# Three rotating PSUM banks each for scores and for transposed scores in the exact attentions of a four-layer cross-attention kernel

## The chip, the cores and the metric

The kernel runs on one core of a Trainium2 chip. The metric is the device time of one execution in microseconds (us): 1616.45 us before the change, the median of three runs that lie between 1616.28 and 1617.36. Five engines work side by side and meet only at semaphores: TensorE (PE; its weight loads are a row of their own, PEld), VectorE (DVE), ScalarE (ACT), GpSimd (POOL) and SyncE (SP), which here only issues transfers. PSUM, into which TensorE writes, has eight banks of 512 fp32 values per partition.

## The reference

A batch of four sequences of 512 tokens, 128 features wide, goes through four layers, and each layer also attends to a context of 154 rows. The change touches the three "exact" attentions, which have 16 heads of 8 features:

```python
# layer 0: cross attention with a padding mask over the 154 context rows
# layer 1: causal self attention over 512 tokens, then cross attention to the context
scores = jnp.einsum('bqhd,bkhd->bhqk', Q, Kp) / jnp.sqrt(jnp.float32(HD))
if causal:
    scores = jnp.where(mask, scores, -jnp.inf)
a = jax.nn.softmax(scores, axis=-1)
o = jnp.einsum('bhqk,bkhd->bqhd', a, V).reshape(Bq, Sq, Dm)
return o @ wo + bo
```

What follows (a mixture of experts, two attentions on 8-bit codes, a gated feed-forward, a grouped attention with rotary positions and a last feed-forward) is left as it is.

## The kernel before

Work on the exact attentions is cut into 12 units, one sequence of one attention each: units 0 to 3 are the padded cross attention (L0), 4 to 7 the causal self attention, 8 to 11 the second cross attention. A unit has 4 groups of 4 heads.

The scores are computed twice. First with queries on the partitions, only to find the maximum of each row: this is a **score step** (`scores_exact` on PE, `top_exact` on DVE), which covers two heads and one tile of 128 queries (two tiles in a cross unit). A cross unit has 16 of them and a self unit 32; in a self unit the widths fall, because of the causal mask, from 512 keys per head over 384 and 256 to 128. All in all there are 256 steps. PE writes the two heads of a step to the two banks of `score[0]` or `score[1]`, in turn, and then counts up `scores_ready`. DVE takes the maximum over both heads in one `tensor_reduce` (line 1960) and counts up `top_ready`. Before step s PE waits until the maximum of step s-2 is taken (line 1099).

Then the scores are computed again with keys on the partitions and the negative maxima added by a further matmul (`scores_transposed`). One **block** is 128 x 512 such transposed scores in one bank of `trans`; a cross group has 5 blocks and a self group 10. PE makes the blocks in pairs w and w+1 (the fifth of a cross group by itself, lines 1137 and 1139), and ACT takes the exponential of each block (line 1509) and counts up `expT_ready`. Before a pair PE waits until the exponentials of all blocks before w are done (line 1130). `weigh_batch` (lines 1175 and 1177) then multiplies the exponentials by the values.

The order is written out by hand. PE, ACT and DVE walk over the same slots, one for each block. PE does in slot w: the transposed pair if w is even within its group, the score steps that `STEPS_OF_SLOT` puts there (they are those of the next group), the items of the slot, and the weighing of a finished batch. In a self group of ten slots the steps stand in slots 8 and 9 (512 keys per head), 0 and 1 (384), 3 and 4 (256) and 5 and 6 (128), so that three times in a group two steps follow each other on PE without a pair between them: in slots 8 and 9, 0 and 1, and 4 and 5. In a cross group of five slots they stand in slots 3 and 4 and in 0 and 1.

Items are the projections and norms of the units around: `K`, `Q`, `V` are projections, `N1`, `r` and `N2` the inversion of the sums (four reciprocals on DVE, line 1727) and the product with them (line 1731), `W` the output projection, then the row statistics on DVE (lines 1633 to 1643), a power on POOL (line 2134), `M` the normalisation on DVE (line 1659) and `H` its transposition (line 941). `tops` transposes the maxima of a group (line 989). The stacked queries and keys of the next unit go through DRAM and come back by transfers that SP issues (lines 800 to 818); the first score step of a unit waits for them.

Of the kernel before, what the change touches and what calls it, by code (L numbers as in the profile page):

```python
# [7 lines left out]
P = 128  # L8
# [387 lines left out]
def build(nc, io, out):  # L396
# [3 lines left out]
    with ctx:  # L400
# [173 lines left out]

        score = [ctx.enter_context(nc.psum_tensor(f"score{i}", [P, 2, 512], fp32)) for i in range(2)]
        trans_pair = ctx.enter_context(nc.psum_tensor("trans", [P, 2, 512], fp32))
        trans = [trans_pair[:, i, :] for i in range(2)]
        acc = ctx.enter_context(nc.psum_tensor("acc", [P, 512], fp32))
        misc = ctx.enter_context(nc.psum_tensor("misc", [P, 512], fp32))
# [203 lines left out]
        with nc.Block() as block:  # L783
# [145 lines left out]
            def _(pe):  # L929
# [152 lines left out]
                def scores_exact(u, i):  # L1082
# [13 lines left out]
                    if u == 0 and i == PER_GROUP[0]:  # L1096
                        pe.wait_ge(q_stacked, 32 * len(Q_TERMS))
                    if at_step >= 2:
                        pe.wait_ge(top_ready, at_step - 1)

                    banks = [(half_rows(s), score[at_step % 2][:, s, :]) for s in range(2)]
                    if is_cross(u):
                        for j in range(2):
                            t, of = 2 * n + j, slice(j * CTX, (j + 1) * CTX)
                            for r, bank in banks:
                                ins = nc.tensor.matmul(bank[:, of], q_stack[r, u % 2, c, t * P:(t + 1) * P],  # L1106
                                                       k_stack_ctx[r, u % 2, c, 0:CTX], start=True, stop=(stage(u) != L0))
                            if stage(u) == L0:
                                for r, bank in banks:
                                    ins = nc.tensor.matmul(bank[:, of], ones_pad[r, :], pad_rows[r, u % 2, :],  # L1110
                                                           start=False, stop=True)
                    else:
                        width = P * (n + 1)
                        for r, bank in banks:
                            nc.tensor.matmul(bank[:, 0:width], q_stack[r, u % 2, c, n * P:(n + 1) * P],
                                             k_stack[r, u % 2, c, 0:width], start=True, stop=False)
                        for h in range(2):
                            for r, bank in banks:
                                ins = nc.tensor.matmul(bank[:, width - P:width], unit_halves[r, h, :], causal[r, h, :],
                                                       start=False, stop=(h == 1))  # L1120
                    ins.then_inc(scores_ready, 1)

                def scores_transposed(w):
# [5 lines left out]
                    if w >= 2:  # L1129
                        pe.wait_ge(expT_ready, blocks[-1] - 1)  # L1130
                    if w == 0 or BLOCKS[w - 1][1] != g:
                        pe.wait_ge(misc_read, out_of("tops", u, g))
                    if len(blocks) == 1:
                        bank = trans[w % 2]
                        pe.wait_ge(k_tail_ready, seq(u) + 1 + (B if stage(u) == CROSS else 0))
# [6 lines left out]
                    for n in range(len(pieces)):  # L1142
                        _, k, q0, c0 = pieces[n]

                        two = [(j, half_rows(j % 2), 2 * g + j // 2, trans[z % 2][:, c0:c0 + TOKENS - q0])
                               for z in blocks for j in [BLOCKS[z][3][n][0]]]
# [80 lines left out]

                pe.wait_ge(top_ready, EXACT_STEPS)
                pe.wait_ge(expT_ready, EXACT_SLOTS)
# [169 lines left out]
            def _(act):  # L1399
# [96 lines left out]
                for w, (u, g, _, pieces) in enumerate(BLOCKS):  # L1496
# [10 lines left out]
                    if n == 0 and stage(u) == L0:  # L1507
                        act.wait_ge(pad_ready, u + 1)
                    nc.scalar.activation(expT[w % SLOTS], trans[w % 2][:, :], ACT.Exp, bias=bias)\  # L1509
                        .then_inc(expT_ready, 1)  # L1510
# [112 lines left out]
            def _(dve):  # L1623
# [326 lines left out]
                def top_exact(u, i):  # L1950
                    c, n = exact_steps(u)[i]
                    at_step = STEP_BASE[u] + i
                    dve.wait_ge(scores_ready, at_step + 1)
                    tops = minus_top[:, :].rearrange("p (t h) -> p h t", h=HEADS)[:, 2 * c:2 * c + 2, :]
                    if is_cross(u):
                        dst = tops[:, :, 2 * n:2 * n + 2]
                        src = score[at_step % 2][:, :, 0:2 * CTX].rearrange("p s (j k) -> p s j k", j=2)
                    else:
                        dst, src = tops[:, :, n], score[at_step % 2][:, :, 0:P * (n + 1)]
                    nc.vector.tensor_reduce(dst, src, axis=AX.X, op=ALU.max, negate=True).then_inc(top_ready, 1)  # L1960

                def split_tops(u, g):
# [3 lines left out]
                    to = top_cols[:, g % 2, :, :, :].rearrange("p t (s z) c -> p t z s c", s=2)  # L1966
                    dve.wait_ge(top_ready, STEP_BASE[u] + PER_GROUP[u] * (g + 1))
                    if GROUPS * u + g >= 2:
# [155 lines left out]
            def _(pool):  # L2124
# [15 lines left out]
                def item(name, u, n=None):  # L2140
# [10 lines left out]
                    elif name == "pads":  # L2151
# [6 lines left out]
                        if b >= 2:  # L2158
                            pool.wait_ge(top_ready, STEP_BASE[b - 1])
                        then(nc.gpsimd.tensor_scalar(pad_col_add[:, b, :], pad_col[:, b, :], -1.0, 1.0e10, ALU.add, ALU.mult))  # L2160
# [205 lines left out]
```

## Time and profile before

| | |
|---|---|
| median of three runs | 1616.45 us |
| the profiled execution | 1629.24 us |
| its span | 1627.4 us |
| exact attentions | about 33 to 594 us of the span |
| of these the self units | about 205 to 432 us |
| score steps (maxima on DVE) | 256 |
| blocks (exponentials on ACT) | 320 |

The profiled execution is 1.84 us longer than its span, which is what lies around it, and 12.8 us (0.8%) longer than the median. PE is the busiest engine in the exact attentions; DVE is second. After 594 us none of the changed lines runs. In a row of the timeline the first number is the start, the second how long the row's instructions took from the first start to the last end, and what stands in brackets is how long the engine had been idle before and who released it.

### The profile page before, as it was taken

What the parts mean: (1) busy time and instruction counts of PE and PEld (TensorE: products, weight loads), DVE (VectorE), ACT (ScalarE), POOL (GpSimd) and SP (SyncE); (2) the same over time, 40 slices, a digit from 0 to 9 for tenths busy, and PEclk for the clock granted to TensorE, in tenths of its full rate; (3) what the DMA queues carried; (4) which work ended last, traced back from release to release, by engine and by line L of the source; (5) the groups of instructions that cost most, each with busy time, mean ns of one, the idle gap of its engine ahead of it and who ended that gap; (6) DMA issues with size and microseconds to landing.
All of it is one profiled execution on the core that took longest, in us unless ns stands there. A gap on an engine that the chain in (4) does not pass through costs nothing.

```text
span 1627.4 us, 28786 instructions
## 1 busy us (share of the span) xinstructions
PE 1109.7 (68%) x9344; PEld 600.2 (37%) x9344; DVE 1109.3 (68%) x3126; ACT 895.0 (55%) x2546; POOL 681.6 (42%) x1054
## 2 busy tenths in 40 slices
PE   2688888787777679784435354444439787898888
PEld 1333344444322238681111121122215544453545
DVE  2577777777666666277989899877765556666533
ACT  1344455545543346347767688888872344545542
POOL 3321010111011323456888888877771245354420
PEclk9899999999998999796555555555559889999999
DMA  6223242022172111217546566655650112111000
GB/s 175 62 47 72 49 120 92 10 72 48 32 150 42 35 41 52 74 40 182 116 95 111 97 110 118 120 109 107 106 106 1 26 40 53 33 28 46 3 1 26
DMA packets 263829, 115.86 MB, mean 71 GB/s; under 512 B 216056, under 2 KB 252544, under 8 KB 261504
## 3 DMA queue, kind: packets, MB, share of 16 engines
q1 hardware_dynamic: 258720, 107.61, 31.6%
q0 software_dynamic: 2048, 4.20, 0.9%
q10 hardware_dynamic: 2912, 2.22, 0.5%
q8 instruction: 75, 1.23, 0.3%
q14 instruction: 74, 0.61, 0.1%
HBM read 38.80 MB, written 16.45 MB: 34 GB/s over the span
## 4 chain that ended last, share of the span: by engine, by line
PE 35%; POOL 19%; issue 17%; DVE 15%; ACT 10%; DMA 2%; SPq 1%; POOLq 0%; another core or an unknown queue 0%; ACTq 0%; DVEq 0%
POOL arena L2268 10%; ACT arena L1562 5%; PE acc L1177 3%; PE trans L1149 2%; POOL inv_total L2257 2%; PE misc L999 2%; PE misc L1005 2%; PE trans L1301 2%; ACT arena L1509 2%; POOL arena L2215 2%; PE score L1313 2%; PE score L1315 2%; PE trans L1155 2%; PE acc L1175 1%; DVE arena L1727 1%
## 5 line engine op out<-in xcount | busy, mean ns | idle before, releaser
L2268 POOL TENSOR_SCALAR arena<-arena,inv_total 128x512 f16<-128x512 f32 (+1 forms) x512 | 302.6, 591 | 55.8 <-DVE inv_total L2038 15.4
L1960 DVE TENSOR_REDUCE minus_top<-score 128x4 f32<-128x616 f32 (+4 forms) x256 | 201.4, 803 | 140.9 <-PE score L1110 54.6
L2134 POOL TENSOR_TENSOR rstd<-spread,minus_half 128x4 f32<-128x4 f32 x36 | 37.7, 1048 | 526.1 <-DVE spread L1643 456.9
L1562 ACT ACTIVATE arena<-score,minus_top,exp_scale 128x512 f32<-128x512 f32 (+1 forms) x340 | 210.6, 626 | 18.1 <-POOL arena L2268 8.1
L1509 ACT ACTIVATE arena<-trans 128x512 f32<-128x512 f32 x240 | 134.5, 596 | 113.8 <-PE trans L1155 107.8
L1600 ACT ACTIVATE arena<-arena,minus_top 128x154 f32<-128x154 f32 x256 | 105.1, 412 | 133.0 <-DVE minus_top L2103 132.9
L1258 PE MATMUL score<-arena 32*128 32x512 bf16 (+1 forms) x340 | 69.0, 458 | 144.1 <-ACT arena L1562 143.2
L2044 DVE TENSOR_REDUCE top_score<-score 128x2 f32<-128x1024 f32 (+1 forms) x128 | 135.7, 1061 | 0.6 <-PE score L1258 0.5
L2288 POOL TENSOR_TENSOR arena<-arena,inv_total 128x512 f32<-128x512 f32 x64 | 66.7, 1041 | 147.4 <-DVE inv_total L2111 133.6
L1562 ACT ACTIVATE arena<-trans,minus_top,exp_scale 128x154 f32<-128x154 f32 (+1 forms) x172 | 105.6, 621 | 16.2 <-POOL arena L2268 11.8
L2098 DVE CUSTOM_DVE_ANT_0 arena<-score,arena 128x154 f32<-128x154 f32 x256 | 66.0, 314 | 62.8 <-PE score L1338 62.4
L2027 DVE TENSOR_SCALAR arena<-arena 128x1024 bf16<-128x1024 f16 x192 | 102.7, 535 | 5.5 <-DMA arena<-arena 5.5
L1553 ACT ACTIVATE minus_top<-top_score,exp_scale 128x2 f32<-128x2 f32 (+1 forms) x192 | 56.5, 294 | 61.4 <-DVE top_score L2044 61.1
L1258 PEld LDWEIGHTS score<-arena 32*128 32x128 bf16 x340 | 14.3, 102 | 195.4 <-ACT arena L1562 178.0
L1177 PE MATMUL acc<-arena 128*32 128x512 f32 (+3 forms) x768 | 80.6, 507 | 4.7 <-issue 4.0
L1258 PE MATMUL trans<-arena 32*128 32x154 bf16 (+1 forms) x172 | 34.7, 451 | 72.0 <-ACT arena L1562 71.8
L1106 PE MATMUL score<-arena 64*128 64x154 bf16 x512 | 45.7, 248 | 54.0 <-issue 32.7
L1527 ACT ACTIVATE arena<-score,arena 128x128 f32<-128x128 f32 x184 | 52.0, 372 | 50.4 <-PE score L1214 43.4
L1277 PE MATMUL acc<-arena 128*32 128x128 bf16 x1536 | 59.2, 307 | 27.8 <-DVE oT L2052 15.2
L1509 ACT ACTIVATE arena<-trans,arena 128x512 f32<-128x512 f32 x80 | 52.3, 687 | 30.6 <-PE trans L1155 27.0
L2044 DVE TENSOR_REDUCE top_score<-trans 128x2 f32<-128x1024 f32 (+1 forms) x64 | 67.4, 1053 | 0.0
L1447 ACT COPY arena<-misc 128x512 bf16<-128x512 bf16 x48 | 28.1, 586 | 70.1 <-PE misc L989 67.3
(282 smaller groups left out, 2902.6 us busy)
## 6 DMA issues: line engine op xcount, KB each, us to landing
arena<-q_terms SPq DMA_DIRECT2D x176, 64.0 KB
late<-arena SPq DMA_DIRECT2D x128, 64.0 KB, 2.0
q_terms<-arena SPq DMA_DIRECT2D x36, 128.0 KB
late<-k_terms SPq DMA_DIRECT2D x64, 64.0 KB
arena<-arena SPq DMA_TRANSPOSE x192, 3.1
by_expert<-zeros SPq DMA_DIRECT2D x2, 1472.0 KB, 17.6
arena<-by_expert SPq DMA_DIRECT2D x10, 256.0 KB, 3.0
from_expert<-arena SPq DMA_DIRECT2D x10, 256.0 KB
```

The lines of the kernel that those rows point to most:

```text
L1177: ins = nc.tensor.matmul(acc[32 * j:32 * j + 32, q0:TOKENS], v_cols[:, k, 4 * g + j, :], src, start=(b % half == 0 and k == 0), stop=(last ...
L1258: ins = nc.tensor.matmul(quant_score[i % 3][:, j, z * n:(z + 1) * n], qT_codes[r:r + 32, u % 2, t * P:(t + 1) * P], k4_codes[r:r + 32, u % ...
L1277: ins = nc.tensor.matmul(acc[32 * j:32 * j + 32, P * t:P * (t + 1)], vals[:, 4 * j + i, :], pT_codes[:, (2 * n + j // 2) % CODE_SLOTS, j % ...
L1509: nc.scalar.activation(expT[w % SLOTS], trans[w % 2][:, :], ACT.Exp, bias=bias)\
L1562: ins = nc.scalar.activation(probs[:, i % 3, j, of], quant_score[i % 3][:, j, of], ACT.Exp, bias=minus_top[:, at_col:at_col + 1], scale=ex ...
L1600: ins = nc.scalar.activation(gq_exp_p[:, i % 3, h, :], shifted[:, i % 3, h, :], ACT.Exp, bias=minus_top[:, at_col:at_col + 1], accum_out=t ...
L1960: nc.vector.tensor_reduce(dst, src, axis=AX.X, op=ALU.max, negate=True).then_inc(top_ready, 1)
L2027: nc.vector.tensor_scalar(pT_codes[:, of, :, :].rearrange("p k q -> p (k q)"), pT_raised[:, of, :, :].rearrange("p k q -> p (k q)"), -HALF ...
L2044: nc.vector.tensor_reduce(of_step(top_score, i), src, axis=AX.X, op=ALU.max, negate=True).then_inc(quant_top, 1)
L2098: ins = nc.vector.tensor_tensor_reduce(out=shifted[:, i % 3, h, :], in0=score[i % 2][:, odd, z * CTX:(z + 1) * CTX], in1=mask_add[:, b % 2 ...
L2268: ins = nc.gpsimd.tensor_scalar(codes[:, (i - 1) % CODE_SOURCES, j, to], probs[:, (i - 1) % 3, j, of], inv_total[:, at_col:at_col + 1], HA ...
L2288: nc.gpsimd.tensor_tensor(gq_p[:, v % 2, :, :], gq_exp_p[:, v % 3, :, 0:P], inv.to_broadcast([P, 4, P]), ALU.mult)
```

## The change

The six banks of `score` and `trans` become one tensor of six banks, and the other stages go on using the same places in it. In the exact attentions the split is now 3 and 3. Head h of the running count of heads (two per step) goes to score bank h mod 3, and block w to transposed bank w mod 3. DVE takes a maximum for each head by itself, 512 `tensor_reduce` in place of 256, and `top_ready` counts heads. PE makes both heads of a step as before and signals once. Before step s it waits for `2 * at_step - 1` maxima, which is up to and including the first head of step s-1. Before a pair it waits for one exponential fewer than before.

```diff
-        score = [ctx.enter_context(nc.psum_tensor(f"score{i}", [P, 2, 512], fp32)) for i in range(2)]
-        trans_pair = ctx.enter_context(nc.psum_tensor("trans", [P, 2, 512], fp32))
+        banks = ctx.enter_context(nc.psum_tensor("banks", [P, 6, 512], fp32))
+        score = [banks[:, 2 * i:2 * i + 2, :] for i in range(2)]
+        trans_pair = banks[:, 4:6, :]
         trans = [trans_pair[:, i, :] for i in range(2)]
+        score_bank = [banks[:, i, :] for i in range(3)]
+        trans_bank = [banks[:, 3 + i, :] for i in range(3)]
...
-                    if at_step >= 2:
-                        pe.wait_ge(top_ready, at_step - 1)
-                    banks = [(half_rows(s), score[at_step % 2][:, s, :]) for s in range(2)]
+                    if at_step:
+                        pe.wait_ge(top_ready, 2 * at_step - 1)
+                    heads = [(half_rows(s), score_bank[(2 * at_step + s) % 3]) for s in range(2)]
...
                     if w >= 2:
-                        pe.wait_ge(expT_ready, blocks[-1] - 1)
+                        pe.wait_ge(expT_ready, blocks[-1] - 2)
...
-                        two = [(j, half_rows(j % 2), 2 * g + j // 2, trans[z % 2][:, c0:c0 + TOKENS - q0])
+                        two = [(j, half_rows(j % 2), 2 * g + j // 2, trans_bank[z % 3][:, c0:c0 + TOKENS - q0])
...
-                    nc.scalar.activation(expT[w % SLOTS], trans[w % 2][:, :], ACT.Exp, bias=bias)\
+                    nc.scalar.activation(expT[w % SLOTS], trans_bank[w % 3], ACT.Exp, bias=bias)\
...
-                    if is_cross(u):
-                        dst = tops[:, :, 2 * n:2 * n + 2]
-                        src = score[at_step % 2][:, :, 0:2 * CTX].rearrange("p s (j k) -> p s j k", j=2)
-                    else:
-                        dst, src = tops[:, :, n], score[at_step % 2][:, :, 0:P * (n + 1)]
-                    nc.vector.tensor_reduce(dst, src, axis=AX.X, op=ALU.max, negate=True).then_inc(top_ready, 1)
+                    for s in range(2):
+                        bank = score_bank[(2 * at_step + s) % 3]
+                        if is_cross(u):
+                            dst, src = tops[:, s, 2 * n:2 * n + 2], bank[:, 0:2 * CTX].rearrange("p (j k) -> p j k", j=2)
+                        else:
+                            dst, src = tops[:, s, n:n + 1], bank[:, 0:P * (n + 1)]
+                        nc.vector.tensor_reduce(dst, src, axis=AX.X, op=ALU.max, negate=True).then_inc(top_ready, 1)
```

The other waits on `top_ready` are only recounted (all heads of the same steps as before). On PE no instruction is added, removed or moved. On DVE every maximum becomes two. This is DVE in a self unit, from the reciprocals of the unit before to the statistics of its output, before the change (`late` and `arena` are SBUF areas, `score` the PSUM banks):

```order
L1727 RECIPROCAL arena<-arena 128x128 [waits misc_read] x2
L1960 TENSOR_REDUCE minus_top<-score 128x2 [waits scores_ready]
L1727 RECIPROCAL arena<-arena 128x128 [waits misc_read]
L1960 TENSOR_REDUCE minus_top<-score 128x2 [waits scores_ready]
L1731 TENSOR_TENSOR oT<-misc,arena 128x512 [waits sums_inverted,misc_raised]
L1960 TENSOR_REDUCE minus_top<-score 128x2 [waits scores_ready]
L1739 TENSOR_TENSOR y<-misc,x 128x512 [waits x_ready,misc_raised]
```

And the same place after it:

```order
L1733 RECIPROCAL arena<-arena 128x128 [waits misc_read] x2
L1967 TENSOR_REDUCE minus_top<-banks 128x1 [waits scores_ready]
L1967 TENSOR_REDUCE minus_top<-banks 128x1
L1733 RECIPROCAL arena<-arena 128x128 [waits misc_read]
L1967 TENSOR_REDUCE minus_top<-banks 128x1 [waits scores_ready]
L1967 TENSOR_REDUCE minus_top<-banks 128x1
L1737 TENSOR_TENSOR oT<-misc,arena 128x512 [waits sums_inverted,misc_raised]
L1967 TENSOR_REDUCE minus_top<-banks 128x1 [waits scores_ready]
L1967 TENSOR_REDUCE minus_top<-banks 128x1
L1745 TENSOR_TENSOR y<-misc,x 128x512 [waits x_ready,misc_raised]
```

The order of the work is the same; each reduction stands as two of one column each, the second without a wait.

## Rows read from the trace of the kernel before

**Rows 1.** Stretches: length, busy PE, PEld, DVE, ACT, POOL; clock, DMA share, GB/s.

```profile
205.00:432.00 227.00, 183.19 (x2494) 96.22 (x2494) 167.35 (x362) 119.35 (x220) 18.17 (x20) 0.99 0.23 61
33.00:205.00 172.00, 134.10 (x1074) 58.45 (x1070) 112.97 (x256) 76.48 (x129) 33.36 (x57) 0.90 0.30 60
432.00:594.00 162.00, 118.12 (x747) 46.43 (x743) 107.15 (x334) 66.61 (x127) 33.20 (x40) 0.91 0.34 72
```

**Rows 2.** Waits of PE in the self units (205 to 432 us).

```profile
PE trans L1149 <- ACT arena L1509: 25.2, 27, 1.2
```

**Rows 3.** Waits of PE in the cross units, 33 to 205 and 432 to 594 us.

```profile
PE score L1106 <- issue: 14.0, 3, 6.4
...
PE score L1106 <- issue: 18.7, 3, 7.3
```

**Rows 4.** Groups by line and shape, the maxima: count, busy us, mean ns.

```profile
L1960 DVE TENSOR_REDUCE minus_top<-score 128x2 f32<-128x1024 f32 x32 | 37.7, 1205 | 11.7 <-PE score L1119 11.7
...
L1960 DVE TENSOR_REDUCE minus_top<-score 128x2 f32<-128x512 f32 x32 | 21.6, 688 | 12.6 <-PE score L1119 12.4
L1960 DVE TENSOR_REDUCE minus_top<-score 128x2 f32<-128x256 f32 x32 | 13.4, 420 | 11.5 <-PE score L1119 11.3
```

**Rows 5.** Timeline of one self group, 305 to 317 us.

```profile
305.36 0.28 PE L1119 MATMUL score<-masks 64*128 64x128 bf16 x4
...
305.68 2.36 DVE L1960 TENSOR_REDUCE minus_top<-score 128x2 f32<-128x1024 f32 x2 [0.80 <-PE score L1119]
305.90 0.39 PE L1115 MATMUL score<-late,arena 64*128 64x512 bf16 x2
...
308.05 0.28 PE L1119 MATMUL score<-masks 64*128 64x128 bf16 x4
...
308.16 0.33 PE L1115 MATMUL score<-late,arena 64*128 64x384 bf16 x2
...
309.99 1.09 ACT L1509 ACTIVATE arena<-trans 128x512 f32<-128x512 f32 x2 [0.81 <-PE trans L1155]
311.13 0.34 PE L1149 MATMUL trans<-arena,late 64*128 64x384 bf16 x2 [0.96 <-ACT arena L1509]
...
311.91 0.28 PE L1119 MATMUL score<-masks 64*128 64x128 bf16 x4
...
312.02 0.22 PE L1115 MATMUL score<-late,arena 64*128 64x128 bf16 x2
...
315.30 0.28 PE L1149 MATMUL trans<-arena,late 64*128 64x256 bf16 x2 [1.01 <-ACT arena L1509]
...
316.72 0.39 PE L1115 MATMUL score<-late,arena 64*128 64x512 bf16 x2
```

**Rows 6.** Timeline where DVE's items precede the maxima, 278 to 290 us.

```profile
278.38 0.39 PE L1115 MATMUL score<-late,arena 64*128 64x512 bf16 x2
...
278.92 1.16 DVE L1960 TENSOR_REDUCE minus_top<-score 128x2 f32<-128x1024 f32 x1
...
287.58 0.27 PE L1115 MATMUL score<-late,arena 64*128 64x256 bf16 x2
...
288.53 1.28 DVE L1960 TENSOR_REDUCE minus_top<-score 128x2 f32<-128x512 f32 x2
...
288.76 0.63 PE L941 MATMUL misc<-ident,normed 128*128 128x128 f32 x4 [0.80 <-DVE normed L1659]
...
289.32 0.10 PEld L1115 LDWEIGHTS score<-late,arena 64*128 64x128 bf16 x2 [0.17 <-DVE minus_top L1960]
```

**Rows 7.** Timeline of a cross unit behind its transfer wait, 460 to 470 us.

```profile
460.50 0.44 PE L1106 MATMUL score<-arena 64*128 64x154 bf16 x4 [7.31 <-issue]
...
464.55 0.43 PE L1106 MATMUL score<-arena 64*128 64x154 bf16 x8
464.89 1.51 DVE L1960 TENSOR_REDUCE minus_top<-score 128x4 f32<-128x616 f32 x2 [0.92 <-PE score L1106]
...
469.77 0.39 PE L1149 MATMUL trans<-arena 64*128 64x512 bf16 x2 [0.45 <-ACT arena L1509]
```

More of the change, by code:

```diff
@@ L1104, in scores_exact @@
                             t, of = 2 * n + j, slice(j * CTX, (j + 1) * CTX)
-                            for r, bank in banks:
+                            for r, bank in heads:
                                 ins = nc.tensor.matmul(bank[:, of], q_stack[r, u % 2, c, t * P:(t + 1) * P],
@@ L1108, in scores_exact @@
                             if stage(u) == L0:
-                                for r, bank in banks:
+                                for r, bank in heads:
                                     ins = nc.tensor.matmul(bank[:, of], ones_pad[r, :], pad_rows[r, u % 2, :],
@@ L1113, in scores_exact @@
                         width = P * (n + 1)
-                        for r, bank in banks:
+                        for r, bank in heads:
                             nc.tensor.matmul(bank[:, 0:width], q_stack[r, u % 2, c, n * P:(n + 1) * P],
@@ L1117, in scores_exact @@
                         for h in range(2):
-                            for r, bank in banks:
+                            for r, bank in heads:
                                 ins = nc.tensor.matmul(bank[:, width - P:width], unit_halves[r, h, :], causal[r, h, :],
@@ L1133, in scores_transposed @@
                     if len(blocks) == 1:
-                        bank = trans[w % 2]
+                        bank = trans_bank[w % 3]
                         pe.wait_ge(k_tail_ready, seq(u) + 1 + (B if stage(u) == CROSS else 0))
@@ L1226, in down @@
                     ins.then_inc(down_raised, 1)
-                pe.wait_ge(top_ready, EXACT_STEPS)
+                pe.wait_ge(top_ready, 2 * EXACT_STEPS)
                 pe.wait_ge(expT_ready, EXACT_SLOTS)
@@ L1966, in split_tops @@
                     to = top_cols[:, g % 2, :, :, :].rearrange("p t (s z) c -> p t z s c", s=2)
-                    dve.wait_ge(top_ready, STEP_BASE[u] + PER_GROUP[u] * (g + 1))
+                    dve.wait_ge(top_ready, 2 * (STEP_BASE[u] + PER_GROUP[u] * (g + 1)))
                     if GROUPS * u + g >= 2:
@@ L2158, in item @@
                         if b >= 2:
-                            pool.wait_ge(top_ready, STEP_BASE[b - 1])
+                            pool.wait_ge(top_ready, 2 * STEP_BASE[b - 1])
                         then(nc.gpsimd.tensor_scalar(pad_col_add[:, b, :], pad_col[:, b, :], -1.0, 1.0e10, ALU.add, ALU.mult))
```

## The prediction

> **What bounds the kernel now.** The changed lines run only in the exact attentions, so busy shares over the whole span decide nothing, and I read the busy time by stretch first. PE is busy 183.2 of 227 us in the self units (81%), 78% in the L0 units and 73% in the second cross attention; DVE is busy 74%, 66% and 66% [rows 1]. PE walks its list in order, so what it waits for is what a gain must come from. The waits by line give that directly: in the self units PE stands 25.2 us, 27 times, in front of a transposed pair until ACT has finished the exponentials [rows 2]. In the cross units the large entry is another: three waits of 14.0 us and three of 18.7 us in all in front of a score step [rows 3]. The profile only calls them "issue", but each is the first step of a unit, behind which the stacked keys and queries come back from DRAM, so I take them for waits on transfers. The timeline of one self group shows the pattern. It comes again after 10.82 us (the step at 305.90 and the one at 316.72), and in it the pairs at 311.13 and at 315.30 stand 0.96 and 1.01 us waiting, the other three in the group do not stand [rows 5].
>
> **What the third transposed bank gives.** A pair now needs one exponential fewer. Two exponentials in a row take 1.09 us, so one is 0.54 us [rows 5]. A pair that stood 0.96 or 1.01 us will stand about 0.45. In all self units this gives at most 27 times 0.54 = 14.6 us, for the 27 waits of [rows 2]. Not all of it arrives. In the second group of each unit the pairs follow on H and W items that are themselves late (below), so I count four pairs a unit in groups three and four and none in the second: 4 x 0.54 = 2.2 us a unit. In the first group one pair stands too, but the next thing that PE needs is a maximum for which DVE is late anyway (278.92 [rows 6]), so that gain is lost.
>
> **What the third score bank costs.** Here the count of banks misleads. Before, two steps could be in flight, in four banks. Now a step still fills two banks and there are three, so a step shares a bank with the step directly before it. PE must wait until DVE has taken the first maximum of that step. Where a pair, a batch or a large item stands between two steps this is hidden; where two steps are neighbours it is not. The wait is: DVE starts 0.04 us after the last matmul of the first step (305.36 + 0.28 = 305.64 against 305.68 [rows 5]), takes the first head, and PE gets going again 0.10 us after the end of a maximum (288.53 + 0.69 = 289.22 against the weight load at 289.32, with 688 ns for that shape [rows 4, 6]).
>
> One head of 512 keys is the size of the 128x512 row, 0.69 us; of 256 keys the 128x256 row, 0.42 us; 384 keys lie halfway, 0.55 us [rows 4]. So:
> - Slots 8 and 9, 512 keys: the next step starts at 305.64 + 0.04 + 0.69 + 0.10 = 306.47 in place of 305.90: +0.57.
> - Slots 0 and 1, 384 keys: 308.33 + 0.69 = 309.02 in place of 308.16: +0.86.
> - Slots 4 and 5, 256 keys: 312.19 + 0.56 = 312.75 in place of 312.02: +0.73.
>
> The ends of matmuls are modelled, and the first part of a step overlapped with the one before, so the lower bound of each takes off 0.08, 0.24 and 0.18: 0.49, 0.62 and 0.55. A plain self group then pays 1.66 to 2.16 us and gets back 1.08. It becomes 0.6 to 1.1 us longer, on 10.8.
>
> Counted for a unit of four groups: in slots 4 and 5 of the first group the V item lies between the steps, in slots 10 and 11 the W item, in 14 and 15 H, and slots 8 and 9 of the first group are priced in the next part. There remain three neighbours of 512 keys, three of 384 and two of 256, in total 3 x 0.57 + 3 x 0.86 + 2 x 0.73 = 5.75 us, or 4.4 us at the lower prices.
>
> **Where DVE is late.** In the second group DVE has reciprocals, a product and the row statistics between the maxima. The second step of 512 keys started at 278.38, while the first maximum did not start before 278.92 [rows 6]. After the change it has to wait until 278.92 + 0.69 + 0.10 = 279.71: +1.33 us. What stands behind it on PE is the N2 item, and behind that the product on DVE, the W item, the statistics, POOL's power, the normalisation and H, one chain. Further on, the step at 287.58 will need the first half of the maximum that started at 288.53: 288.53 + 0.42 + 0.10 = 289.05, then its own 0.3 us, so H, which is in line behind it, starts at 289.35 or later and not at 288.76: +0.6. Together 1.9 us, of which I take 1.8, since part of the second lateness is the first one seen again; bounds 1.2 and 2.3.
>
> **The split itself.** Two maxima of half the size take longer than one: 2 x 0.688 - 1.205 = 0.17 us and 2 x 0.420 - 0.688 = 0.15 us [rows 4]. For 256 steps that is 41 us of DVE. In the self units DVE rises from 167.4 to 188 of 227 us (83%), still beside PE. Its price is in the chain above only where DVE is late; I take 0.1 us a unit in addition. At worst, were DVE the bound, all 20 us of the self units would count. The Trainium skill ("Perfetto Trace Analysis", section "Optimizing Scalar/DVE Operations") gives about 125 ns of fixed cost for a DVE instruction that reads PSUM, and the trace's 150 to 170 ns is near it and decides.
>
> **Self units.** 5.75 + 1.8 + 0.1 - 2.2 = 5.4 us a unit at the upper prices, and 4.4 + 1.2 - 2.2 = 3.4 at the lower. I take 4.5, 18 us for four units, with ends at 13 and 24 (the last with the 2.3).
>
> **Cross units.** What PE does ahead of the wait for transfers is free in both directions, up to the 7.31 us of the row at 460.50 [rows 7]. What counts is from there to the next unit's Q item. There one neighbouring couple of steps (464.55, both in one row of 8 matmuls) will pay: DVE starts at 464.89, one head of 2 x 154 values takes 0.49 us (a line through 256 and 512 values [rows 4]), 464.89 + 0.49 + 0.10 = 465.48 against a second step that began about 464.7: +0.8. The pair at 469.77 waited 0.45 us for an exponential, and that goes [rows 7]. With 0.1 us more on DVE before the parts of Q this is +0.3 to +0.4 a unit, and 2 us for the seven units (bounds 0 and 5). Unit 0 has the same couples with nothing to win at the start: +1. Unit 11 has hardly any steps left and only wins: -1.
>
> **Sum.** 18 + 2 + 1 - 1 = +20 us. It is made against the profiled execution of 1629.24 us (span 1627.4 and 1.84 around it). The median of the runs is 0.8% shorter, which changes 20 us by 0.2, so: 1616.45 + 20 = 1636.
>
> **Against this speaks a rule.** The Trainium skill ("Perfetto Trace Analysis", sections "Optimization Strategy" and "Optimizing Scalar/DVE Operations") says that a gap that keeps returning on the engine that should be full can mean too little PSUM for the next tile, and that breaking up an instruction of an engine that is not full may let others go on sooner. For the pairs the trace agrees (0.96 and 1.01 us each time). For the scores there are no such gaps of PE now, so there is nothing that a maximum per head could give back.
>
> **The rivals.**
> - *The pairs win.* If the new stalls of the steps fall where PE would have stood for ACT anyway, and the third bank gives what it can: 14.6 us from [rows 2] less some 5 us of stalls that stay. That would be 1616 - 10 = 1606. For it speaks that PE's largest wait is this one. Against it speaks the order: between slots 0 and 1 and the pair that stood (slot 4) lie a batch and a full pair, and ACT starts later by as much as that pair does. This is the rule above as a mechanism. 0.10.
> - *Even.* Stalls of steps are at the lower prices, DVE's chain in the second group hides its own lateness, and all five standing pairs a unit win: 4 x (4.4 - 2.7) = 7, less what the first group absorbs, 4 to 7, gives 0 to 3 us: 1618. 0.07.
> - *DVE becomes the bound in the self units.* It decides once PE's stalls push DVE's items behind the maxima so that both wait for each other through the whole unit: the 20 us of the split come on top of half of the rest, +32: 1648. For it speaks 83% busy with an in-order list; against it, that DVE still idles before most maxima of a plain group (0.80 us at 305.68 [rows 5]). 0.10.
> - *The score rotation does nothing.* One signal for both heads could make three banks as good as two steps in flight, if DVE were always ahead. The couples of [rows 5] exclude it: DVE cannot take a maximum before it is there. Chance 0.
>
> **How the numbers follow.** The forecast has 0.73, with a range of its own of 1627 to 1646. A change under 0.2% (3.2 us) cannot be told from none here. Faster 0.10, within 0.07, slower 0.83. The range for 8 in 10 leaves out the pairs' victory and the far half of the case of DVE: 1617 to 1648.
>
> **What would show it.** Right: the waits list of PE gains an entry of score steps on DVE's maxima of 25 to 40 us with some 50 or more waits, and the entry of pairs on ACT falls from 25.2 to 10 to 14 us in the self units; the self units as a whole grow by 13 to 24 us, and a plain group goes from 10.8 to between 11.4 and 11.9; the maxima are 512 with 20% more busy time; nothing changes behind 594 us but the start. Wrong: if plain groups stay at 10.8, the neighbours are covered by something that I did not see; if DVE no longer idles before maxima in plain groups, it is the bound; if the cross units shift by more than 1 us each, the transfer wait was not the limit there.

## The result, and the profile after

The changed kernel takes 1646.67 us (median of four runs, 1645.34 to 1656.61); the kernel before, timed beside it, 1616.37 us. The ratio is 1.0191, with an interval of 1.0150 to 1.0231. Timed again it was 1.0152 (1.0091 to 1.0214). Some executions of a kernel are slower as a whole; ratios and the differences of medians leave them out, among them one of the changed kernel at 3471.51 us. The change makes the kernel slower, as forecast; the forecast of 1636 us had +20 us in it, the medians show +30 and +25, and the two profiled executions lie 16.1 us apart (1629.24 and 1645.34).

Where the time went is read from three starts of the profile after: the first score step, the first transposition of the experts (the end of the exact attentions) and the first score of the quantised attention behind the experts. Columns are start, length, engine, line, operation, output and inputs.

```profile
32.29 0.31 PE L1111 MATMUL banks<-arena 64*128 64x154 bf16 x2 [15.29 <-DMA arena<-q_terms]
615.59 0.63 PE L1210 MATMUL acc<-ident,arena 128*128 128x128 f32 x4 [0.77 <-ACT arena L1491]
753.35 0.61 PE L1264 MATMUL banks<-arena 32*128 32x512 bf16 x6 [0.70 <-issue]
```

Before, the same three stand at 32.68, 597.12 and 736.88. From the first to the second it was 564.4 us and is now 583.3: +18.9. From the second to the third it was 139.8 and is 137.8. So the loss lies in the exact attentions, and the stages behind them give nothing to it. Within, I use one length for all kernels from here on, the **self stretch**: from the start of the pair in slot 0 of the first self unit to the last full pair of the fourth. It is 214.7 us before (205.25 to 419.98), 214.7 in a second profile of the kernel before, 233.1 after (208.89 to 442.02) and 235.8 in a second profile of the changed kernel. So +18.4 and +21.0 stand there.

What PE waited for in the exact attentions after the change, by line (in total, times, longest):

```profile
PE banks L1120 <- DVE minus_top L1967: 35.2, 45, 1.7
PE banks L1111 <- DMA arena<-q_terms: 31.0, 4, 15.3
PE banks L1111 <- DVE minus_top L1967: 22.4, 35, 1.6
PE banks L1111 <- issue: 14.0, 2, 9.7
PE banks L1155 <- ACT arena L1515: 10.4, 20, 0.7
```

L1120 and L1111 are score steps (self and cross), L1155 the pairs. The entry that [rows 2] had, 25.2 us of pairs in front of ACT, has fallen to 10.4. In its place stand 35.2 us of self steps in front of a maximum, and 22.4 us in cross units. The transfer waits of [rows 3] are still there, partly under another name (q_terms).

The maxima, which were [rows 4], by shape (busy us, mean ns of one, then the idle time before them):

```profile
L1967 DVE TENSOR_REDUCE minus_top<-banks 128x2 f32<-128x308 f32 x256 | 109.1, 468 | 89.8 <-PE banks L1115 53.7 <-PE banks L1111 35.5
L1967 DVE TENSOR_REDUCE minus_top<-banks 128x1 f32<-128x512 f32 x64 | 40.7, 677 | 5.1 <-PE banks L1124 4.9
L1967 DVE TENSOR_REDUCE minus_top<-banks 128x1 f32<-128x384 f32 x64 | 32.7, 552 | 14.4 <-PE banks L1124 13.5
L1967 DVE TENSOR_REDUCE minus_top<-banks 128x1 f32<-128x256 f32 x64 | 24.1, 418 | 12.2 <-PE banks L1124 12.2
L1967 DVE TENSOR_REDUCE minus_top<-banks 128x1 f32<-128x128 f32 x64 | 15.5, 284 | 15.4 <-PE banks L1124 14.5
```

One head's duration is what the forecast took (0.69, 0.55 and 0.42 us against 677, 552 and 418 ns). But 64 times 677 ns is 43.3 us and the busy time is 40.7: two maxima in a row overlap. All of them are busy 222.0 us against 201.4 before, 10% more and not 20%. DVE idles before every shape, so it isn't the bound.

A plain self group after, the rows of PE in which it stood (they answer to [rows 5]; the number in brackets is the wait):

```profile
312.85 0.34 PE L1155 MATMUL banks<-arena,late 64*128 64x384 bf16 x2 [0.47 <-ACT arena L1515]
314.43 0.23 PE L1120 MATMUL banks<-late,arena 64*128 64x128 bf16 x2 [0.53 <-DVE minus_top L1967]
317.22 0.28 PE L1155 MATMUL banks<-arena,late 64*128 64x256 bf16 x2 [0.53 <-ACT arena L1515]
319.18 0.39 PE L1120 MATMUL banks<-late,arena 64*128 64x512 bf16 x2 [0.46 <-DVE minus_top L1967]
322.26 0.34 PE L1120 MATMUL banks<-late,arena 64*128 64x384 bf16 x2 [0.66 <-DVE minus_top L1967]
324.62 0.34 PE L1155 MATMUL banks<-arena,late 64*128 64x384 bf16 x2 [0.47 <-ACT arena L1515]
```

From one group's pair to the next group's it is 11.77 us against 10.82. The pairs stand 0.47 and 0.53 in place of 0.96 and 1.01, and the second step of each of the three couples (slots 4 and 5, 8 and 9, 0 and 1) stands 0.53, 0.46 and 0.66 us where none stood.

The place in the first group where DVE is late ([rows 6] shows it before), now:

```profile
285.66 0.28 PE L1155 MATMUL banks<-arena,late 64*128 64x256 bf16 x2 [0.53 <-ACT arena L1515]
288.86 0.39 PE L1120 MATMUL banks<-late,arena 64*128 64x512 bf16 x2 [1.70 <-DVE minus_top L1967]
289.29 3.00 PE L1003 MATMUL misc<-arena 128*128 128x512 f32 x4
292.22 1.69 PE L1183 MATMUL acc<-arena 128*32 128x384 f32 x16
```

And the same stretch in windows (PE busy, weight loads, DVE, ACT, POOL, then the granted clock, DMA share, GB/s):

```profile
287.00:289.00 2.00, 0.30 (x5) 0.11 (x4) 2.00 (x4) 1.22 (x3) 0.00 (x0) 1.00 0.52 135
289.00:291.00 2.00, 2.00 (x9) 0.92 (x6) 2.00 (x4) 0.00 (x0) 0.00 (x0) 0.78 0.51 139
291.00:293.00 2.00, 2.00 (x10) 0.34 (x12) 1.06 (x2) 0.00 (x0) 0.00 (x0) 0.50 0.52 139
293.00:295.00 2.00, 2.00 (x32) 0.95 (x25) 0.14 (x2) 0.40 (x1) 0.00 (x0) 0.87 0.51 135
```

PE works 0.30 us of the two before 289, and then the granted clock falls from 1.00 to 0.50 (from the 2.4 to the 1.2 GHz level). The N2 item and the batch behind it take 3.00 and 1.69 us here. The same place in the first self unit of the same profile has the same wait, and there the clock stays at 1.00 and they take 1.98 and 1.07:

```profile
228.28 0.39 PE L1120 MATMUL banks<-late,arena 64*128 64x512 bf16 x2 [1.70 <-DVE minus_top L1967]
228.71 1.98 PE L1003 MATMUL misc<-arena 128*128 128x512 f32 x4
230.62 1.07 PE L1183 MATMUL acc<-arena 128*32 128x384 f32 x16
```

Of the four waits of 1.70 us in this profile the second and the third are followed by a fall of the clock, the first and the fourth are not. The forecast had not priced this.

### The profile page after: what moved, and what is told of

It is laid out like the page before. It is cut to its first block, busy times and chain, and to the rows that moved or that the text cites. A ratio compares the mean times of both kernels' runs of the same rounds, so it can differ in the third digit from the quotient of the medians.

```text
span 1643.5 us, 29042 instructions
## 1 busy us (share of the span) xinstructions
PE 1112.0 (68%) x9344; PEld 594.9 (36%) x9344; DVE 1127.2 (69%) x3382; ACT 893.9 (54%) x2546; POOL 679.7 (41%) x1054
## 4 chain that ended last, share of the span: by engine, by line
PE 34%; POOL 19%; DVE 18%; issue 14%; ACT 9%; DMA 4%; SPq 2%; POOLq 0%; DVEq 0%; ACTq 0%
POOL arena L2275 10%; ACT arena L1568 5%; DVE minus_top L1967 3%; PE acc L1183 3%; DMA arena<-q_terms 3%; POOL inv_total L2264 2%; PE misc L1003 2%; PE misc L1009 2%; PE banks L1155 2%; PE banks L1307 2%; PE banks L1319 2%; PE banks L1321 2%; DVE top_score L2051 1%; SPq L811 1%; PE banks L1120 1%
## 5 line engine op out<-in xcount | busy, mean ns | idle before, releaser
L1568 ACT ACTIVATE arena<-banks,minus_top,exp_scale 128x512 f32<-128x512 f32 (+1 forms) x512 | 315.9, 624 | 33.9 <-POOL arena L2275 19.3
L1967 DVE TENSOR_REDUCE minus_top<-banks 128x2 f32<-128x308 f32 (+4 forms) x512 | 222.0, 476 | 136.9 <-PE banks L1115 53.7
L1264 PE MATMUL banks<-arena 32*128 32x512 bf16 (+1 forms) x512 | 101.8, 455 | 215.3 <-ACT arena L1568 214.0
L1515 ACT ACTIVATE arena<-banks 128x512 f32<-128x512 f32 x240 | 134.5, 596 | 130.4 <-PE banks L1161 125.7
L2051 DVE TENSOR_REDUCE top_score<-banks 128x2 f32<-128x1024 f32 (+1 forms) x192 | 203.1, 1058 | 0.6 <-PE banks L1264 0.5
L2105 DVE CUSTOM_DVE_ANT_0 arena<-banks,arena 128x154 f32<-128x154 f32 x256 | 65.9, 313 | 58.0 <-PE banks L1344 57.5
L1568 ACT ACTIVATION_READ_ACCUMULATOR arena<-banks,minus_top,exp_scale 128x1 f32 x512 | 100.3, 196 | 0.0
L1111 PE MATMUL banks<-arena 64*128 64x154 bf16 x512 | 46.9, 245 | 68.3 <-DMA arena<-q_terms 31.0
L1533 ACT ACTIVATE arena<-banks,arena 128x128 f32<-128x128 f32 x184 | 52.2, 369 | 42.7 <-PE banks L1220 42.6
L1515 ACT ACTIVATE arena<-banks,arena 128x512 f32<-128x512 f32 x80 | 52.3, 687 | 33.7 <-PE banks L1161 31.3
L1161 PE MATMUL banks<-arena 64*128 64x512 bf16 (+3 forms) x384 | 64.0, 329 | 0.0
L1120 PE MATMUL banks<-late,arena 64*128 64x512 bf16 (+3 forms) x256 | 39.3, 303 | 36.3 <-DVE minus_top L1967 35.2
```

What stands on the lines that cost most here:

```text
L1161: ins = nc.tensor.matmul(to, ones[r, j, :], top_rows[r, g % 2, q0:TOKENS], start=False, stop=True)
L1264: ins = nc.tensor.matmul(quant_score[i % 3][:, j, z * n:(z + 1) * n], qT_codes[r:r + 32, u % 2, t * P:(t + 1) * P], k4_codes[r:r + 32, u % ...
L1515: nc.scalar.activation(expT[w % SLOTS], trans_bank[w % 3], ACT.Exp, bias=bias)\
L1568: ins = nc.scalar.activation(probs[:, i % 3, j, of], quant_score[i % 3][:, j, of], ACT.Exp, bias=minus_top[:, at_col:at_col + 1], scale=ex ...
L2051: nc.vector.tensor_reduce(of_step(top_score, i), src, axis=AX.X, op=ALU.max, negate=True).then_inc(quant_top, 1)
L2105: ins = nc.vector.tensor_tensor_reduce(out=shifted[:, i % 3, h, :], in0=score[i % 2][:, odd, z * CTX:(z + 1) * CTX], in1=mask_add[:, b % 2 ...
```

## The experiments

Each ratio is against the kernel before, timed beside it. The edits of E1 and E2 on the kernel before do all of the change but the rotation of the banks, so what is left from E2 to the changed kernel is the third transposed bank.

**E1, the split alone.** Kernel before, four score banks, one maximum per head, the wait for the whole step two back:

```
-   pe.wait_ge(top_ready, at_step - 1)
+   pe.wait_ge(top_ready, 2 * (at_step - 1))
-   nc.vector.tensor_reduce(dst, src, ...).then_inc(top_ready, 1)       # both heads
+   for s in range(2): nc.vector.tensor_reduce(dst, src of head s, ...).then_inc(top_ready, 1)
```

> The kernel before with one thing of the change: one maximum per head (512 reductions in place of 256). Four score banks, two transposed banks, and PE waits for all of step s-2 as before. My theory (the price is PE's wait for the step directly before): +1 to +5 us against the kernel before, where DVE is late anyway. Rival A (the additional DVE instructions are the price): +12 to +20 us, most of what the profiled executions differ by (16 us). Rival B (something behind the exact attentions, since the medians differ by 30 us and the profiled executions by 16): 0.

Measured: ratio 1.0015 (0.999 to 1.004), self stretch 214.5 us against 214.7, plain group 10.83. 256 more instructions on DVE cost nothing there. That refutes DVE's additional work as the cause.

**E2, the wait added.** E1 with the wait of the changed kernel, though the fourth bank is still there:

```
-   if at_step >= 2: pe.wait_ge(top_ready, 2 * (at_step - 1))
+   if at_step:      pe.wait_ge(top_ready, 2 * at_step - 1)
```

> The kernel before with a maximum per head, and PE waits before step s for the first maximum of step s-1, as in the changed kernel, though there are four score banks and it need not. Two transposed banks. My theory: this holds the whole loss and none of the gain, so it is slower than the changed kernel: +22 to +30 us against the kernel before, PE waiting some 60 us for maxima. Rival A: as e1. If the third transposed bank is worth nothing: equal to the changed kernel.

Measured: ratio 1.021 (1.017 to 1.025), self stretch 236.4 (+21.7), plain group 12.75. Its waits:

```profile
PE score L1115 <- DVE minus_top L1961: 33.4, 45, 1.7
PE trans L1149 <- ACT arena L1509: 24.6, 31, 1.2
PE score L1106 <- DVE minus_top L1961: 17.1, 30, 1.1
```

The pairs wait as before, and the steps stand on the maxima 45 times in the self units, as often as after the change. One line of waiting makes the whole loss and more; what three transposed banks change in it is the difference between E2 and the changed kernel: 236.4 against 233.1 (235.8 in the second profile of the changed kernel, below).

**The two kernels again.** A second profile of the kernel before, and the changed kernel timed and profiled again:

> The kernel before, unchanged, for a profile on the same chip as the runs of this call. Both theories: self units of 55 to 56 us each (from V item to V item), exact attentions of 564 us from the first score step to the first transposition of the experts on the earlier chip, and on a chip with slower transfers up to 8 us more in the cross units, as the profile of e1 has them.

> The changed kernel, unchanged, in five rounds beside the others. My theory: 1.0% to 1.5% slower than the kernel before (16 to 25 us), since the two profiles differ by 16 us and only the exact attentions by 18.5; the 30 us between the medians were partly chance. Rival B (a loss behind the exact attentions): 1.9% again, and the profile shows the later stages longer than in before_again.

Measured: the self stretch repeats (214.7; 235.8 against 233.1). The rest of the exact attentions doesn't: first score step to experts is 565.9 us before and 596.4 after the second time, +30.5, of which +21.0 is the self stretch and +9.5 the rest, where the first pair of profiles had +18.4 and +0.5. The rest has two halves that behave differently. From the first score step to the self stretch (the L0 units) it is 172.6 us before and 176.6 after, and 174.0 and 178.4 the second time: about +4 in both. Behind the self stretch it goes both ways: 177.1 and 173.6, then 177.2 and 182.2. And the clock fell at all four N2 items this time (2.9 us or more each for 1.98), where the first profile had it at two.

**E3 and E4, the batch between the pair and the steps.** If neighbouring steps are what costs, something between them should give it back. E3 is the changed kernel, E4 the kernel before, both with:

```
     scores_transposed(w)
+    weigh_batch(...)      # when slot w has one
     for u, i in steps_in_slot(w): scores_exact(u, i)
     for it in EXACT_ITEMS.get(w, ()): item(*it)
-    weigh_batch(...)
```

> The changed kernel (three and three banks), and in each slot PE does the finished batch ahead of the score steps and not behind them and the items. The batches stand in the second slot of each couple of neighbours, so one of 0.6 to 1 us now lies between the two steps. My theory: the stalls of 0.46 to 0.66 us at the couples go, the waits for DVE in the second group of a unit stay, and the gain of the third transposed bank stays: 8 us faster to 5 us slower than the kernel before, 12 to 25 us faster than the changed one. Rival A (instructions of DVE): within 3 us of the changed kernel.

> The kernel before (four score banks, two transposed) with the batches ahead of the score steps in each slot, as in e3. A control for e3: what the reordering does by itself. My theory: no neighbour waits here in the kernel before, so -2 to +3 us. The difference of e3 to it is what the split of the banks costs or gives once the couples are parted.

Measured: E3 1.0148 (1.0114 to 1.0182), E4 1.0106 (1.007 to 1.0142). Both are misses: the order alone costs the kernel before 1%, which I had expected to be free, and E3 is not near the kernel before. E4's waits show where:

```profile
PE score L1106 <- issue: 35.9, 6, 10.8
PE misc L989 <- DVE arena L1974: 24.3, 16, 3.8
```

L989 is the `tops` item, which transposes the maxima of a group, and L1974 the last DVE instruction that prepares them. In the kernel before it waits 6.5 us in all, 8 times, since a batch of 2 us stands between the last step of a group and this item in a cross unit; in E4 that batch stands ahead of the step, nothing of its length is left to cover the maxima, and the wait is 24.3 us, 16 times. The waits for transfers (the first entry) are 35.9 us against 32.7. That is another reason than the one the expectation of E5 below gives, an item Q that feeds the transfers. The self stretch is 221.4 us in E4 and 217.3 in E3, so with a batch between them the steps on 3 and 3 banks are no longer the slower ones there. As a whole the split costs +0.4% against its own partner (E3 to E4), within their intervals. That supports the reason, in a kernel that is no use; the next pair confines the order to the self units.

**E5 and E6, steps parted in the self units only.** In slots 1, 5 and 9 of a self group the batch, or the slot's K or N2 item, goes ahead of the steps; everywhere else the order is as it was. E5 is the changed kernel, E6 the kernel before.

```
+  if stage(u) == SELF and in_slot % 10 in (1, 5, 9) and in_slot != 11:
+      if slot has K or N2: order = items, steps, batch
+      else:                order = batch, steps, items
```

> The changed kernel with the neighbouring steps parted in the self units alone: in slots 1, 5 and 9 of ten PE does the batch first, or, where the slot has a K or N2 item, that item first. The cross units keep the order of the changed kernel, because e3 and e4 put their batch of 2 us in front of the Q item that feeds the transfers. My theory: self units of 54 to 56 us, against 60 to 61.5 of the changed kernel, so 14 to 22 us faster than it and within 6 us of the kernel before. Rival A (instructions of DVE): self units stay above 59 us.

> The kernel before (four score banks, two transposed) with the order of e5 in the self units. Control for e5. My theory: nothing to part here, plain groups stay within 0.3 us of 10.82, and the time within 4 us of the kernel before. If the order by itself gives something, this beats the kernel before.

Measured: E5 1.0047 (1.0011 to 1.0083), self stretch 215.5; E6 1.0035 (1.0005 to 1.0066), self stretch 217.6. A plain group of E5, the rows that stood:

```profile
310.07 0.34 PE L1155 MATMUL banks<-arena,late 64*128 64x384 bf16 x2 [0.18 <-ACT arena L1522]
313.75 0.28 PE L1155 MATMUL banks<-arena,late 64*128 64x256 bf16 x2 [0.53 <-ACT arena L1522]
317.48 0.34 PE L1120 MATMUL banks<-late,arena 64*128 64x384 bf16 x2 [0.25 <-DVE minus_top L1974]
320.27 0.34 PE L1155 MATMUL banks<-arena,late 64*128 64x384 bf16 x2 [0.18 <-ACT arena L1522]
```

10.20 us from pair to pair, where the changed kernel needs 11.77 and the kernel before 10.82. Only one of the three step waits is left, 0.25 us. The same banks and the same maxima with the steps apart lose 0.8 us in the self stretch in place of 18.4. The order by itself doesn't give that: E6, its partner with the old banks, has a plain group of 10.72 us (10.82 before) and a self stretch 2.9 us longer than the kernel before. That shows that the neighbouring steps are the cause. Above the kernel before E5 still lies by about 8 us, and not in the self units: its L0 units take 180.9 us against 174.0. (In one first group of E5 the clock fell too, 22.04 us against 20.40 in the next unit.)

**E9, E5 with two transposed banks** (`% 3` to `% 2`, and the wait one exponential stricter):

> e5 with two transposed banks in turn in place of three, and the wait of the kernel before for them. It shows what the third transposed bank is worth once the couples are parted. My theory: two pairs a plain group wait 0.54 us longer each, or less where parting has moved them, so a plain group goes from 10.20 to between 10.8 and 11.3 us, and the kernel is 3 to 10 us slower than e5. Rival (the gain comes back as waits elsewhere, as between e2 and the changed kernel in the first group): within 2 us of e5.

Measured: 1.0128 (1.0081 to 1.0175), self stretch 220.9, plain group 11.16. The third transposed bank is worth 0.96 us a plain group and 5.4 us in the self stretch here. Against E6, from which it differs only in the score banks and the maxima, E9 is 3.3 us longer in the self stretch: that is what the wait for the step before still costs with the steps apart, where it costs 21.9 (E1 to E2) with neighbours.

**E7 and E8, a signal for each head.** PE does one head after the other, each with its own wait (`head - 2`) and its own signal to DVE; so PE waits for the head three back instead of the first head of the step before. E7 is that on the changed kernel, E8 on E5.

```
+  for s in range(2):
+      head = 2 * at_step + s
+      if head >= 3: pe.wait_ge(top_ready, head - 2)
+      one_head(..., score_bank[head % 3]).then_inc(scores_ready, 1)
```

> The changed kernel with PE doing one head after the other, each with its own wait (for the head three before) and its own signal. My theory: the share of a bank with the step directly before matters only for the second head now, and DVE starts earlier; the stall of a couple falls from about 0.5 to 0.2 us or less, but heads no longer run side by side in the two halves of the rows, which lengthens a step by 0.1 to 0.25 us: self units of 57 to 60 us, 0 to 12 us faster than the changed kernel. Rival A: no difference to the changed kernel beyond 2 us.

> e5 and e7 together: three and three banks, couples parted in the self units, and one wait and one signal a head. The best candidate with three and three. My theory: plain groups of 10.0 to 10.3 us as in e5, and the places where DVE is late cost less, as in e7 (21.4 in place of 23.0 us in the first group): 2 to 6 us faster than e5, so within 4 us of the kernel before. Rival: the heads one after the other lengthen each step by more than they save, and it is slower than e5.

Measured: E7 1.013 (1.0068 to 1.0192), self stretch 230.1, plain group 11.74 (11.77 without it). E8 1.005 (1.0018 to 1.0081), self stretch 212.6, plain group 10.13. In the plain group the finer signals give next to nothing; E7's gain of 3 us is in the first groups (21.4 us in place of 23.05), where the clock did not fall and N2 took 1.98 us. E8 has the shortest self stretch of all, 2.1 us under the kernel before, and is still not faster than it as a whole. No version tried beats the kernel before.

**E11, PE kept busy ahead of the late maximum.** The changed kernel with eight matmuls of no use in slot 9 before the N2 item:

```
+  if slot w has N2 and stage(u) == SELF:
+      pe.wait_ge(expT_ready, w - 1)
+      for _ in range(8): nc.tensor.matmul(trans_bank[(w + 1) % 3], q_stack..., q_stack..., start=True, stop=True)
```

> The changed kernel with eight needless matmuls (128 x 512, into the free transposed bank, overwritten by the next pair) in slot 9 of each self unit, in the place where PE waits up to 1.70 us for DVE's late maximum. In the changed kernel the granted clock falls to 0.50 behind that wait (289 to 293 us), the N2 product takes 3.00 us and the batch 1.69, against 1.98 and 1.07 in e2. Theory of the clock: with the wait filled it stays at 1.00, the stretch from the pair of slot 0 to that of slot 10 goes from 23.0 to 21.4 us in the two middle units, 3 to 5 us in all. Rival (the products are slow for another reason, such as transfers): both stay at 3.00 and 1.69 us, and the filling costs nothing or its own time.

Its rows at that place, and behind them the same place in E2, where PE stands 1.22 us and nothing fills it:

```profile
289.84 1.90 PE L1199 MATMUL banks<-arena 64*128 64x512 bf16 x8
292.04 1.98 PE L1003 MATMUL misc<-arena 128*128 128x512 f32 x4
293.96 1.07 PE L1183 MATMUL acc<-arena 128*32 128x384 f32 x16
```

```profile
297.41 0.39 PE L1115 MATMUL score<-late,arena 64*128 64x512 bf16 x2 [1.22 <-DVE minus_top L1961]
297.84 1.98 PE L999 MATMUL misc<-arena 128*128 128x512 f32 x4
```

Measured: the clock stays at 1.00 at all four N2 items, the first group is 21.4 us in both middle units instead of 23.05, self stretch 230.4 (2.7 less than after). The ratio is 1.0177 (1.0119 to 1.0234), which can't be told from the changed kernel's. So the fall of the clock is shown as the reason for 1.65 us in a first group, and is a small part of the whole. That the wait brings the fall about is shown less firmly: behind 1.70 us of standing it fell six times in eight (two profiles of the changed kernel), behind 1.22 us in E2 and behind the filled wait never in four each.

## Why the prediction was right, and where not

**The cause is the one named.** A step shares a bank with the step directly before it, and where two steps are neighbours PE stands until one maximum is done. E2 makes the loss with that wait alone, E5 removes it by parting the steps, E1 excludes the split. A unit grew by 4.8, 5.9 and 5.4 us between successive V items, forecast 4.5 with bounds 3.4 and 6. The self stretch grew by 18.4 us, forecast 18, and that this is so close is luck: the forecast has four units of 4.5, the stretch three of 5.3 on average and 2.4 us of the last one, most of whose fourth group lies outside it.

**The plain group, term by term.** Forecast for the couples 1.66 to 2.16 us, measured 1.92 (10.83 to 12.75, E1 to E2). Forecast for the pairs -1.08, measured -0.98 (12.75 to 11.77). Together +0.95, forecast 0.6 to 1.1. Prices read from ends and starts of a trace, with the other engine's duration for one head, held within 0.2 us.

**All costs of a unit together.** E2, which has only costs, is longer by 6.2, 6.2 and 5.7 us a unit; the forecast's costs were 7.65 at the upper prices and 5.6 at the lower (4.4 + 1.2). The lower end was nearer, and the couples are not why: in the two plain groups they came to 3.8 us, in the middle of 3.3 to 4.3. The step that was mis-sized is the lateness of DVE, forecast 1.8 us. From E1 to E2 the first group of the second unit grew by 1.73 us (19.67 to 21.40) and the second group by 0.53 (14.47 to 15.00); less the couple in each, 0.66 and 0.46, that leaves 1.1. The first place cost what was forecast (a wait of 1.22 for 1.33), the further 0.6 for H hardly anything.

**The gain of the pairs.** In the plain groups it arrived: from E2 to the changed kernel six of the seven that the stretch holds shrank by 0.98 us and the last by 0.81, 6.7 us in all, where four pairs in each of four units should have given 8.8. In the first group the forecast called it lost, because DVE is late behind it, and where the clock stayed up it was exactly lost (22.68 and 22.74, 20.60 and 20.59 us). Where the clock fell it turned into a loss. PE reached the late maximum sooner, stood 1.70 us and not 1.22, and N2 and its batch took 1.65 us more, in two units of four in one profile and in all in the other. So the self stretch shrank by 3.3 us in the first profile and by 0.7 in the second. This error and the one above cancel only against the upper prices (5.4 us a unit, and 5.3 measured on average); the 4.5 that was taken was too low.

**DVE's busy time** was forecast at +20% over the maxima and rose by 10%, since two of them in a row overlap. The sum had only 0.1 us a unit for it, so the miss changed nothing.

**The other units.** I had given them +2, and the first pair of profiles has +0.5, the second +9.5. The L0 units alone took about 4 us more in both, so their term was too small. The cross steps stand 22.4 us on maxima, and in exchange the waits for transfers behind the very first one are shorter, 29.7 us in all against 36.0 (30.0 against 39.9 in the second pair): part of the new waits is covered, as the forecast had it, but not all. How long the transfers keep PE differs from run to run by more than the term, so the second cross attention is left open, and with it why the medians lie 25 to 30 us apart and the profiled executions 16. The time of 1636 was so 11 us short of the median, inside the range of 1617 to 1648 and just past the 1646 at which the forecast's own range ended. What the runs show is the mechanism in the self units; the share of the other units stays open.

**The rivals.** *The pairs win*: the pairs' wait did fall by 14.8 us (25.2 to 10.4), much as the 14.6 of the forecast, but beside 35.2 us of new waits. In the plain group both kinds of wait stand, so the one doesn't cover the other. *Even* needed the costs at their lower end, and there they nearly were, but also more than the full gain of the pairs, of which 3.3 us of 8.8 were left after the falls of the clock. *DVE the bound* is refuted by E1 and by the idle time before every shape. *The rotation does nothing* is refuted by E2.

## What to carry to other kernels

Count how many units of work can be in flight, not how many buffers there are: three banks with steps that fill two leave one step in flight, where four banks left two. Such a wait costs most where two producers of the same kind stand next to each other in the list (21.9 us here against 3.3 with them apart), and there it can be priced to 0.1 or 0.2 us from one trace; look first at what may stand between them, and at what that had covered where it stood, since a 2 us batch moved away from between the maxima of a group and the item that needs them cost 1% by itself. Before crediting an earlier start, see whether what follows is late anyway: the time doesn't vanish, it becomes an idle stretch of the engine in front.

## What the hardware showed that was not expected

- PE stood 1.70 us, in a stretch of two microseconds in which it worked 0.30, and then the granted clock went from 1.00 to 0.50 for 3 to 4 us; in the same profile the same 1.70 us at 228.28, also with 0.30 us of work in the two before, left it at 1.00, and so did 1.22 us of standing at the same place in E2. The Trainium skill ("TensorE: Matmul & The Clock Gate", section "Part 1: The HAM clock gate") says that the clock follows how busy PE has lately been. The trace agrees in that the falls stand behind the idle stretches and stay away when they are filled (E11), and adds what a fall costs here, 1.65 us, and that the same idle stretch doesn't always bring one.
- Two maxima of 512 values from PSUM, one behind the other, took 1.22 us (the row below) and not twice 677 ns. One over both heads took 1205 ns [rows 4]. So splitting it was nearly free in throughput, and the first half is done after 0.68 us.
- The waits for the stacked keys and queries at the start of a cross unit differ between executions of the same kernel. A length that does not contain them repeats to 0.1 us in the kernel before (the self stretch, 214.7 and 214.7).

The row of DVE in the profile after, at the late place shown above; x2 means two maxima, one per head:

```profile
288.17 1.22 DVE L1967 TENSOR_REDUCE minus_top<-banks 128x1 f32<-128x512 f32 x2
```
